# A hybrid network's kernel: its first two layer norms taken on rows of tokens instead of columns

## The chip, the core and the metric

The kernel runs on one core of a Trainium2 chip. A core has engines with a queue of instructions each, which wait for one another by semaphores: TensorE (PE, matmuls and transposes, writing to PSUM; PEld is its weight load), VectorE (DVE), ScalarE (ACT), GpSimd (POOL) and SyncE (SP, which issues DMAs). The metric is the device time of one execution in microseconds (us), as a median of several.

## The reference

A stack of eight blocks on x of shape (4, 1024, 128), in fp32. The change touches the first one, an RWKV mixer. What matters of it:

```python
def _ln(x, g, b):
    m = x.mean(-1, keepdims=True)
    v = x.var(-1, keepdims=True)
    return (x - m) * jax.lax.rsqrt(v + 1e-05) * g + b
...
xn = _ln(x, ln1_g, ln1_b)
xx = _shift(xn)
xk = xn * tm_mu_k + xx * (1.0 - tm_mu_k)
...
k = xk @ Wk
...
x = x + r * wkv @ Wo
ei = _ln(x, ln2_g, ln2_b)
```

Both x in the last but one line and the x under the first norm are themselves the output of a plain layer norm of the input, so the kernel needs two norms of it: an inner one (the residual) and an outer one on top (the mixer's input). Both come from the same mean and variance, since the norm of a norm is the centred input times another factor. wkv is a recurrence over the 1024 tokens of each of the 4 batches; behind it stands the second norm, and then a mixture of experts.

## The kernel before

The 4096 tokens are eight chunks of 512 (`CH`, `NCH`), two for each batch. Nearly everything is kept with the 128 features on partitions and tokens along the free axis: `X` (the input), `Y` (the residual) and `N` (the normed input, padded by a column on each side of a batch). Three fifths of a large buffer, `big[0]` to `big[2]`, serve first for the loaded rows and later for the recurrence's keys K, values V and gates R. Each engine's program is written out by hand in its order; semaphores such as `ln_out` (one more for each chunk of the norm) are counted up through the whole kernel.

The input comes in five DMAs as rows of tokens (`k.rows`, a token on a partition, 128 features along the free axis). TensorE turns each 128x128 tile (`turn`, line 3039) and VectorE copies a turned chunk out of PSUM to `X` (`keep`, line 2990). Then `TwoNorms` runs on columns, in the order that `layernorm` writes out: TensorE multiplies a chunk by a centring matrix (line 89) and the squares (ScalarE, line 96) by a matrix of 1/128 (line 107), so that each column's variance stands on all partitions. ScalarE takes the logarithm twice and the exponential twice (lines 151 to 155, 512 columns each), one pair for the inner and one for the outer norm. VectorE makes the outer norm in two operations (lines 164 and 167) and the inner one, `Y`, in one (line 165). A batch of vectors (gains, biases, mixing factors) is turned in the middle of it, and GpSimd folds the mixing factors into the weights (`rwkv_loads`, lines 394 and 397).

`wkv` follows. TensorE makes keys, values and gates (`mix`, lines 422 and 423), ScalarE takes them out of PSUM (line 474) and makes the recurrence's weights (lines 486 and 488), and VectorE runs the scans and products (lines 540 to 561). On the way out TensorE sums a denominator (`den`, lines 431 and 434), ScalarE inverts it (`over`, lines 492 and 494), VectorE gates (lines 566 and 569), TensorE multiplies by Wo (`out`, line 441), and VectorE adds the product to the residual (`add`, line 584). The second norm's centring (line 89) stands between these in TensorE's queue.

## Time and profile before

| | |
|---|---|
| median of 3 runs | 1082.73 us (1080.31 to 1083.93) |
| the profiled execution's own time | 1089.32 us |
| its span, from the first to the last instruction | 1087.6 us |
| mean granted TensorE clock | 0.959 |
| busy in the span | PE 990.2 us, DVE 845.5 us, ACT 738.1 us, POOL 376.6 us |

The profile is of one execution, and its times count from the span's start. The stages that the change touches take up the first 130 us: the load and the two first norms until about 37 us, the recurrence until about 115 us, the second norm until about 133 us. The busy shares are means over stages with different limits, so they say little of these. Durations are those that the profiler recorded: an instruction that is held up by something inside its engine counts as longer, and one that waits for a semaphore starts later.

### The profile page before, as it was taken

The numbers are of one execution on the slowest core, as the hardware profiler recorded it, in microseconds if no ns is written. First come the engines' busy times: TensorE is split into PE (matmuls) and PEld (weight loads), VectorE is DVE, ScalarE is ACT, GpSimd is POOL, SyncE is SP. The second block draws the span as 40 slices with busy tenths as digits, with TensorE's granted clock in tenths as the row PEclk, the third lists the DMA queues.
The fourth block names the chain that finished last, engine by engine and source line by source line (L and its number), as shares of the span: only waits on it lengthen the run. The fifth ranks groups of instructions, "written<-read, shape, count | busy, mean of one in ns | idle before, by whom it ended". The sixth has DMA issues, their size and how long they took to land.

```text
span 1087.6 us, 21260 instructions
## 1 busy us (share of the span) xinstructions
PE 990.2 (91%) x7772; PEld 634.4 (58%) x7780; DVE 845.5 (78%) x1541; ACT 738.1 (68%) x1313; POOL 376.6 (35%) x480
## 2 busy tenths in 40 slices
PE   7888999889967999899998999889999899898898
PEld 3333544379953544777663454567776777763476
DVE  4899788768745767777765778899879899799974
ACT  5895656546646358455777457788778878886784
POOL 0100037737661113000000113788768777320210
PEclk9998999989989999899999999899889999999989
DMA  7900035368850000000000000000000000000002
GB/s 196 289 16 1 1 112 160 124 220 273 262 183 11 1 0 11 2 2 2 1 1 1 0 1 10 1 3 2 2 2 2 2 27 2 2 1 1 0 1 78
DMA packets 42686, 54.53 MB, mean 50 GB/s; under 512 B 6251, under 2 KB 29244, under 8 KB 42588
## 3 DMA queue, kind: packets, MB, share of 16 engines
q1 hardware_dynamic: 37968, 42.75, 13.3%
q0 software_dynamic: 4288, 10.46, 2.6%
q8 instruction: 62, 1.02, 0.4%
q14 instruction: 36, 0.29, 0.1%
q10 hardware_dynamic: 332, 0.01, 0.0%
HBM read 22.11 MB, written 20.93 MB: 40 GB/s over the span
## 4 chain that ended last, share of the span: by engine, by line
PE 59%; DVE 18%; ACT 12%; issue 7%; DMA 2%; POOL 2%; SPq 0%; ACTq 0%; DVEq 0%
PE psum L1419 4%; PE psum L1391 3%; PE psum L2608 3%; PE psum L2232 3%; PE psum L89 2%; PE psum L1053 2%; PE psum L1019 2%; DVE N L2829 2%; PE psum L1068 2%; DVE arena L2820 2%; ACT N L2720 2%; PE psum L1879 2%; PE psum L1032 2%; PE psum L2618 2%; PE psum L2149 2%
## 5 line engine op out<-in xcount | busy, mean ns | idle before, releaser
L2720 ACT ACTIVATE N<-N 128x1024 f32<-128x1024 f32 x64 | 67.7, 1058 | 27.4 <-DVE N L2829 26.6
L2608 PEld LDWEIGHTS psum<-arena 32*128 32x128 f32 x1024 | 65.8, 196 | 27.0 <-issue 14.9
L2618 PE MATMUL psum<-ident,N 128*128 128x128 f32 x512 | 73.8, 290 | 7.2 <-POOL N L2789 6.5
L2608 PE MATMUL psum<-arena 32*128 32x128 f32 x1024 | 78.4, 293 | 1.6 <-ACT arena L2698 1.4
L2716 ACT ACTIVATE arena<-psum 128x1024 f32<-128x1024 f32 x64 | 65.7, 1027 | 18.1 <-PE psum L2618 17.6
L882 POOL DMA_INDIRECT out_rows<-mixed,out_index x62 | 60.3, 972 | 38.9 <-DVE arena L958 23.3
L1322 POOL TENSOR_TENSOR arena<-arena 128x512 f32<-128x512 f32 x16 | 20.2, 1260 | 138.3 <-DVE arena L1354 138.3
L2789 POOL TENSOR_TENSOR N<-N,arena 128x512 f32<-128x512 f32 x64 | 67.9, 1060 | 0.0
L2783 POOL TENSOR_TENSOR mixed<-N 128x256 f32<-128x256 f32 x64 | 46.7, 730 | 60.9 <-ACT N L2720 60.2
L2618 PEld LDWEIGHTS psum<-ident,N 128*128 128x128 f32 x512 | 58.1, 146 | 16.2 <-POOL N L2789 9.8
L2788 POOL TENSOR_TENSOR N<-N,arena 128x512 f32<-128x512 f32 x64 | 66.9, 1045 | 0.0
L876 POOL DMA_INDIRECT slot_rows<-arena,slot_index x48 | 50.7, 1057 | 28.7 <-ACT arena L822 15.3
L2819 DVE TENSOR_REDUCE arena<-psum 128x8 f32<-128x512 f32 x64 | 43.9, 686 | 21.1 <-PE psum L2608 20.8
L2389 DVE TENSOR_REDUCE arena<-psum 128x32 f32<-128x1024 f32 x32 | 39.1, 1222 | 26.1 <-PE psum L2232 26.1
L1319 POOL MEMSET arena<- 128x512 bf16 x4 | 2.0, 523 | 161.8 <-DVE N L124 161.8
L96 ACT ACTIVATE ln_sq<-psum 128x512 f32<-128x512 f32 x48 | 28.4, 592 | 41.2 <-PE psum L89 40.2
L2337 ACT ACTIVATE arena<-arena 128x1024 f32<-128x1024 f32 x32 | 33.6, 1051 | 21.6 <-DVE arena L2400 21.3
L1419 PE MATMUL psum<-arena,ffw 128*128 128x512 f32 (+1 forms) x96 | 46.8, 625 | 0.0
L2828 DVE TENSOR_TENSOR N<-psum,arena 128x512 f32<-128x512 f32 x64 | 44.2, 691 | 2.2
L89 PE MATMUL psum<-X,center 128*128 128x512 f32 x64 | 37.5, 674 | 8.0 <-DVE X L1176 3.8
L1472 ACT ACTIVATE arena<-psum 9x512 bf16<-9x512 f32 x16 | 9.4, 585 | 52.1 <-PE psum L1403 52.1
L1391 PE MATMUL psum<-arena,ffw 128*128 128x512 f32 x96 | 44.6, 597 | 0.1
(446 smaller groups left out, 2787.7 us busy)
## 6 DMA issues: line engine op xcount, KB each, us to landing
arena<-weights SPq DMA_DIRECT2D x31, 320.0 KB, 2.7
slot_rows<-zeros SPq DMA_DIRECT2D x1, 8060.0 KB, 26.6
arena<-slot_rows SPq DMA_DIRECT2D x31, 260.0 KB
arena<-tw_rows SPq DMA_DIRECT2D x16, 256.0 KB, 3.7
arena<-out_rows SPq DMA_DIRECT2D x6, 512.0 KB
out_dram<-arena SPq DMA_DIRECT2D x8, 256.0 KB, 2.4
arena<-in_L_attn_a_x_dram SPq DMA_DIRECT2D x3, 512.0 KB, 7.1
weights<-in_L_attn_a_eWk_dram SPq DMA_DIRECT2D x1, 1024.0 KB, 5.8
```

The source lines that it names most:

```text
L89: self.nc.tensor.matmul(k.bank[c % W][:], k.center[:], self.src(c), start=True, stop=True).then_inc(k.ln_centered, 1)
L876: nc.gpsimd.indirect_dma_start(k.slot_rows, at, rows[:, t, :], None).then_inc(k.rt_sent, 16)
L882: nc.gpsimd.indirect_dma_start(k.out_rows, at, made[:, i % 4, j, :], None).then_inc(k.sx_out[i % 4], 16)
L1391: nc.tensor.matmul(k.bank[j][:], k.W1[:, j, :], xm[c], start=True, stop=True).then_inc(k.ff_h, 1)
L1419: op = nc.tensor.matmul(own[c][:], k.W2[0:rows, j, :], hm[0:rows, j * CH:(j + 1) * CH], start=(j == 0), stop=(j == GR - 1))
L2608: op = nc.tensor.matmul(scored[half][:, e * P:(e + 1) * P], k.sg_Q[b % 2][at, seg, 2 * j:2 * j + 2, :].rearrange("p h n -> p (h n)"), k.sg ...
L2618: op = nc.tensor.transpose(turned_to[:, e * P:(e + 1) * P], pr[n % 4][:, e * P:(e + 1) * P], k.ident[:])
L2716: nc.scalar.activation(pT[n % 2], turned_to, ACT.Copy).then_inc(k.sg_pT, 1)
L2720: nc.scalar.activation(pr[n % 4], pr[n % 4], ACT.Exp).then_inc(k.sg_exp, 1)
L2783: nc.gpsimd.tensor_tensor(hs[n % 2], mine[:, :, 0:32], mine[:, :, 32:64], ALU.add).then_inc(k.sg_half, 1)
L2788: nc.gpsimd.tensor_tensor(mine, mine, sm[n % 4][:, 0:8, None].to_broadcast([P, 8, SEG]), ALU.mult)
L2789: nc.gpsimd.tensor_tensor(others, others, spread(sm[n % 4][:, 8:40]), ALU.mult).then_inc(k.sg_mul, 1)
```

## The change

`RowNorms` takes the place of `TwoNorms`. It works on the rows as they were loaded, where a token is a partition (for each of four tiles in a chunk) and its 128 features lie along the free axis, so that mean and variance are single numbers per row, kept in a small buffer `row_stats`. For each chunk VectorE sums the rows and scales the sums to means (`mean_rows`); GpSimd subtracts them (`center_rows`, to `big[1]`); ScalarE squares (`square_rows`, to `big[2]`); VectorE sums the squares (`variance_rows`); ScalarE takes two logarithms of 4 columns and one exponential of 8 (`deviation_rows`). VectorE then makes the outer norm from the raw rows, tile by tile with a subtraction and a multiplication by a scalar per row (`scale_outer`, to `big[2]`), TensorE turns the result (`turn`), and ScalarE applies gain and bias on the way to `N` (`affine`). GpSimd makes the inner norm's rows (`scale_inner`), which stay rows in `Y`. The input is still turned for `X`.

The residual is no longer added by VectorE: in `out`, TensorE adds its eight tiles of a batch to PSUM as products with the identity, which turns them, before the product with Wo; `add` only copies. VectorE, and not GpSimd, folds the mixing weights, behind its last chunk. ScalarE's table for the exponentials is loaded behind the decay's exponential. The values wait for the rows of the residual, because they overwrite the centred rows.

```diff
-class TwoNorms(Norm):
-    def __init__(self, nc, k, src, dst, outer, **kinds):
-        super().__init__(nc, k, src, dst, **kinds)
-        self.outer, self.second0 = outer, k.ln_affine * NCH
+class RowNorms(Norm):
...
+    def raw_turned(self, c):
+        return c + 1 + max(0, c - 3)
+    def scaled_turned(self, c):
+        return c + 1 + min(NCH, c + 4)
+    def spread(self, j, c):
+        return self.stat(j, c)[:, :, None].to_broadcast([P, 4, P])
+    def mean_rows(self, dve, c):
         k, nc = self.k, self.nc
-        at = c % W
+        dve.wait_ge(k.loaded[[first <= c < end for first, end in LOADS].index(True)], 16)
+        nc.vector.tensor_reduce(self.stat(0, c), self.rows(k.big[0], c), AX.X, ALU.add).then_inc(k.x_mean, 1)
+        dve.wait_ge(k.x_mean, 2 * c + 1)
+        nc.vector.tensor_scalar(self.stat(0, c), self.stat(0, c), 1.0 / P, None, ALU.mult).then_inc(k.x_mean, 1)
+    def center_rows(self, pool, c):
+        k, nc = self.k, self.nc
+        pool.wait_ge(k.x_mean, 2 * c + 2)
+        nc.gpsimd.tensor_tensor(self.rows(k.big[1], c), self.rows(k.big[0], c), self.spread(0, c), ALU.subtract).then_inc(k.ln_centered, 1)
+    def turn_x(self, pe, c):
+        k, nc = self.k, self.nc
+        pe.wait_ge(k.loaded[[first <= c < end for first, end in LOADS].index(True)], 16)
+        if c >= 4:
+            pe.wait_ge(k.x_ready, c - 3)
+        rows = self.rows(k.big[0], c)
+        for t in range(4):
+            op = nc.tensor.transpose(k.bank[c % 4][:, t * P:(t + 1) * P], rows[:, t, :], k.ident[:])
+        op.then_inc(k.x_turned, 1)
+    def keep_x(self, dve, c):
+        k, nc = self.k, self.nc
+        dve.wait_ge(k.x_turned, self.raw_turned(c))
+        nc.vector.tensor_copy(plain(k.X, c), k.bank[c % 4][:]).then_inc(k.x_ready, 1)
+    def square_rows(self, act, c):
+        k, nc = self.k, self.nc
+        act.wait_ge(k.ln_centered, c + 1)
+        nc.scalar.activation(plain(k.big[2], c), plain(k.big[1], c), ACT.Square).then_inc(k.ln_squared, 1)
+    def variance_rows(self, dve, c):
+        k, nc = self.k, self.nc
+        dve.wait_ge(k.ln_squared, c + 1)
+        nc.vector.tensor_reduce(self.stat(1, c), self.rows(k.big[2], c), AX.X, ALU.add).then_inc(k.ln_var, 1)
...
+        both = k.row_stats[:, 2:4, 4 * c:4 * (c + 1)]
+        act.wait_ge(k.ln_var, c + 1)
+        nc.scalar.activation(self.stat(2, c), self.stat(1, c), ACT.Ln, scale=1.0 / P, bias=k.eps[:, 0:1])
+        nc.scalar.activation(self.stat(3, c), self.stat(1, c), ACT.Ln, scale=(1.0 + EPS_LN) / P, bias=k.eps_eps[:, 0:1]).then_inc(k.ln_logs, 1)
+        act.wait_ge(k.ln_logs, c + 1)
+        nc.scalar.activation(both, both, ACT.Exp, scale=-0.5).then_inc(k.ln_rstd, 1)
...
+    def scale_outer(self, dve, c):
         k, nc = self.k, self.nc
-        at, bank = c % W, k.bank[c % W][:]
-        out = self.outer(c)
+        dve.wait_ge(k.ln_rstd, c + 1)
+        raw, to = self.rows(k.big[0], c), self.rows(k.big[2], c)
+        for t in range(4):
+            op = nc.vector.tensor_scalar(to[:, t, :], raw[:, t, :], self.stat(0, c)[:, t:t + 1], self.stat(3, c)[:, t:t + 1], ALU.subtract, ALU.mult)
+        op.then_inc(k.ln_scaled, 1)
+    def scale_inner(self, pool, c):
+        k, nc = self.k, self.nc
+        pool.wait_ge(k.ln_rstd, c + 1)
+        nc.gpsimd.tensor_tensor(self.rows(k.Y, c), self.rows(k.big[1], c), self.spread(2, c), ALU.mult).then_inc(k.x_rows, 1)
+    def turn(self, pe, c):
+        k, nc = self.k, self.nc
+        if c >= 4:
+            pe.wait_ge(k.ln_out, PRIMED["ln_out"] + c - 3)
+        pe.wait_ge(k.ln_scaled, c + 1)
+        rows = self.rows(k.big[2], c)
+        for t in range(4):
+            op = nc.tensor.transpose(k.bank[4 + c % 4][:, t * P:(t + 1) * P], rows[:, t, :], k.ident[:])
+        op.then_inc(k.x_turned, 1)
...
+        act.wait_ge(k.x_turned, self.scaled_turned(c))
+        nc.scalar.activation(padded(k.N, c), k.bank[4 + c % 4][:], ACT.Identity, scale=k.ln1[:, 0:1], bias=k.ln1[:, 1:2]).then_inc(k.ln_out, 1)
...
+def row_norms(nc, k, block, norm, feed):
+    turn_vecs, keep_vecs = feed
+    k.ln_done, k.ln_logged = NCH + PRIMED["ln_out"], NCH
+    @block.tensor
+    def _(pe):
+        pe.wait_ge(k.ident_one, 1)
+        for c in range(NCH + 3):
+            if c < NCH:
+                norm.turn_x(pe, c)
+            if c == NCH - 1:
+                turn_vecs(pe)
+            if c >= 3:
+                norm.turn(pe, c - 3)
+    @block.scalar
+    def _(act):
+        activations(act, k, "natural_log_exp_and_others")
+        for c in range(NCH + 2):
+            if c < NCH:
+                norm.square_rows(act, c)
+            if 1 <= c <= NCH:
+                norm.deviation_rows(act, c - 1)
+            if c >= 2:
+                norm.affine(act, c - 2)
+    @block.gpsimd
+    def _(pool):
+        for c in range(NCH + 2):
+            if c < NCH:
+                norm.center_rows(pool, c)
+            if c >= 2:
+                norm.scale_inner(pool, c - 2)
+    @block.vector
+    def _(dve):
+        for c in range(NCH + 2):
+            if c < NCH:
+                norm.mean_rows(dve, c)
+            if c >= 2:
+                norm.scale_outer(dve, c - 2)
+            if 1 <= c <= NCH:
+                norm.keep_x(dve, c - 1)
+                norm.variance_rows(dve, c - 1)
+        keep_vecs(dve)
...
-    @block.gpsimd
-    def _(pool):
-        pool.wait_ge(k.wA_in, 64)
-        pool.wait_ge(k.vecs_ready, 1)
+    @block.vector
+    def _(dve):
+        dve.wait_ge(k.wA_in, 64)
+        dve.wait_ge(k.vecs_ready, 1)
         for j, mu in enumerate(("mu_k", "mu_v", "mu_r")):
-            nc.gpsimd.tensor_scalar(k.wmix[:, j, :], k.wA[:, j, :], k.vec(mu), None, ALU.mult).then_inc(k.mix_fold, 1)
+            nc.vector.tensor_scalar(k.wmix[:, j, :], k.wA[:, j, :], k.vec(mu), None, ALU.mult).then_inc(k.mix_fold, 1)
         for j in range(3):
-            pool.wait_ge(k.mix_fold, j + 1)
-            nc.gpsimd.tensor_tensor(k.wA[:, j, :], k.wA[:, j, :], k.wmix[:, j, :], ALU.subtract).then_inc(k.mix_fold, 1)
+            dve.wait_ge(k.mix_fold, j + 1)
+            nc.vector.tensor_tensor(k.wA[:, j, :], k.wA[:, j, :], k.wmix[:, j, :], ALU.subtract).then_inc(k.mix_fold, 1)
...
-                pe.wait_ge(k.ln_out, normed - NCH + 1 + (W + n if n < W else 2 * b + c))
+                pe.wait_ge(k.ln_out, normed - NCH + 1 + 2 * b + c)
...
+            pe.wait_ge(k.x_rows, 2 * b + 2)
+            for t in range(8):
+                nc.tensor.matmul(backs[b][:, t * P:(t + 1) * P], rows[:, 8 * b + t, :], k.ident[:], start=(t % 4 == 0), stop=False, skip_group_check=True)
             pe.wait_ge(k.wkv_out, b + 1)
             for c in range(2):
-                nc.tensor.matmul(backs[b][:, c * CH:(c + 1) * CH], k.wA[:, 3, :], R[:, half[b][c]], start=True, stop=True).then_inc(k.wkv_prod, 1)
+                nc.tensor.matmul(backs[b][:, c * CH:(c + 1) * CH], k.wA[:, 3, :], R[:, half[b][c]], start=False, stop=True, skip_group_check=True).then_inc(k.wkv_prod, 1)
...
-        activations(act, k, "exp_and_others")
...
+                if kind == "V":
+                    act.wait_ge(k.x_rows, 2 * b + c + 1)
...
+        activations(act, k, "exp_and_others")
...
-                nc.vector.tensor_tensor(k.Y[:, half[b][c]], k.Y[:, half[b][c]], backs[b][:, c * CH:(c + 1) * CH], ALU.add).then_inc(k.wkv_y, 1)
+                nc.vector.tensor_copy(k.Y[:, half[b][c]], backs[b][:, c * CH:(c + 1) * CH]).then_inc(k.wkv_y, 1)
...
-    layernorm(k, block, first, feed)
+    row_norms(nc, k, block, first, feed)
...
+    def turn_vecs(pe):
+        pe.wait_ge(k.x_ready, 5)
+        pe.wait_ge(k.vecs_in, 16 * len(table))
+        nc.tensor.transpose(late[:, 0:len(VROWS)], k.vrows[:], k.ident[0:len(VROWS), 0:len(VROWS)]).then_inc(k.vecs_turned, 1)
```

The first place is VectorE's program of the first norms. In the kernel before, it does this for a chunk, here ahead of the copy of the turned vectors (`vecs`; `N` and `Y` are the two results):

```order
L2990 COPY X<-psum 128x512
L164 SCALAR_TENSOR_TENSOR N<-psum,ln,arena 128x512
L165 TENSOR_TENSOR Y<-psum,ln_std 128x512
L167 TENSOR_SCALAR N<-N,ln 128x512
L3063 COPY vecs<-psum 128x43
```

Three operations out of PSUM and one in place made a chunk of both results and of `X`. In the changed kernel the same engine does this for a chunk in the middle of the stage (line numbers are now the changed kernel's own, and `arena` holds the rows):

```order
L161 TENSOR_REDUCE row_stats<-arena 128x4
L163 TENSOR_SCALAR row_stats<-row_stats 128x4
L211 TENSOR_SCALAR arena<-arena,row_stats 128x128 x4
L183 COPY X<-psum 128x512
L193 TENSOR_REDUCE row_stats<-arena 128x4
```

Only the copy to `X` is left of the former operations; the scalings (line 211) are those of the chunk two ahead of the one that is summed in line 161. The second place is the end of the same stage on VectorE:

```order
L183 COPY X<-psum 128x512
L193 TENSOR_REDUCE row_stats<-arena 128x4
L211 TENSOR_SCALAR arena<-arena,row_stats 128x128 x4
L3157 COPY vecs<-psum 128x43
L505 UNCONDITIONAL_BRANCH
L510 TENSOR_SCALAR mixed<-wA,vecs 128x128 x3
L513 TENSOR_TENSOR wA<-wA,mixed 128x128 x3
```

The copy of the vectors and the folding of the mixing weights have moved behind the last scaling. The third place is TensorE's program on the way out of the recurrence. Before, the sums of batch 2 (lines 431 and 434), the product of batch 0 (line 441) and the sums of batch 3 follow on one another:

```order
L431 MATMUL psum<-ln_std,ident 128x512 x2
L434 MATMUL psum<-ln_sq,ident 128x512 x2
L441 MATMUL psum<-arena,wA 128x512 x2
L431 MATMUL psum<-arena,ident 128x512 x2
L434 MATMUL psum<-arena,ident 128x512 x2
```

Nothing but these stands between the sums. In the changed kernel the former lines 431, 434 and 441 are lines 548, 551 and 561:

```order
L548 MATMUL psum<-ln_std,ident 128x512 x2
L551 MATMUL psum<-ln_sq,ident 128x512 x2
L558 MATMUL psum<-ident,Y 128x128 x8
L561 MATMUL psum<-arena,wA 128x512 x2
L548 MATMUL psum<-arena,ident 128x512 x2
L551 MATMUL psum<-arena,ident 128x512 x2
```

Line 558, the eight tiles of the residual, has come in ahead of the product, and so it does for each of the four batches.

## Rows read from the trace of the kernel before

**Rows 1.** Windows: busy us of each engine (instructions), granted clock, DMA share, GB/s.
```profile
15.00:35.70 20.70, 16.06 (x43) 6.23 (x42) 14.89 (x25) 19.93 (x36) 5.04 (x23) 1.00 0.75 210
90.00:95.00 5.00, 1.98 (x3) 0.83 (x3) 4.93 (x5) 4.69 (x5) 0.00 (x0) 0.76 0.00 0
95.00:100.00 5.00, 5.00 (x8) 2.08 (x7) 4.93 (x5) 1.24 (x2) 0.00 (x0) 0.56 0.00 0
```

**Rows 2.** Chain of waits, end of the first norms: start, us, what.
```profile
35.16 0.53 ACT arena L155
...
38.31 2.30 DVE arena L540
```

**Rows 3.** Chain of waits, the way out of the recurrence.
```profile
93.23 3.78 PE psum L431 x4
...
99.99 1.72 PE psum L441 x4
101.70 1.72 PE psum L431 x4
...
106.85 1.73 PE psum L89 x4
...
112.68 1.95 PE psum L441 x4
```

**Rows 4.** Timeline, two instructions: start, us, engine, line, operation [idle before, releaser].
```profile
6.12 1.28 ACT L46 ACT_TABLE_LOAD   x1 [6.12 <-issue]
...
112.68 0.67 PE L441 MATMUL psum<-arena,wA 128*128 128x512 f32 x1 [0.68 <-DVE arena L569]
```

**Rows 5.** Single lines: count, duration in ns as min/median/max, first and last start, forms.
```profile
L2836 DVE TENSOR_REDUCE arena<-N x64: 673/676/685, 692.0 to 933.9; 128x32 f32<-128x512 f32 x64
L1295 DVE TENSOR_SCALAR ffw<-ffw,W_sum x3: 275/279/285, 347.8 to 348.2; 128x128 f32<-128x128 f32 x2, 96x128 f32<-96x128 f32 x1
L326 DVE TENSOR_SCALAR weights<-weights x3: 169/170/174, 941.6 to 1048.1; 128x4 f32<-128x4 f32 x2, 128x16 f32<-128x16 f32 x1
L2990 DVE COPY X<-psum x8: 682/691/692, 5.8 to 23.9; 128x512 f32<-128x512 f32 x8
L2788 POOL TENSOR_TENSOR N<-N,arena x64: 1035/1045/1061, 693.9 to 936.6; 128x512 f32<-128x512 f32 x64
L271 ACT ACTIVATE mixed<-X x8: 612/624/682, 776.9 to 946.9; 128x512 f32<-128x512 f32 x8
L295 ACT ACTIVATE weights<-psum,eps x7: 244/246/274, 783.2 to 1030.1; 128x4 f32<-128x4 f32 x6, 128x16 f32<-128x16 f32 x1
```

**Rows 6.** Timeline of VectorE at 347.8 us.
```profile
347.84 0.67 DVE L1295 TENSOR_SCALAR ffw<-ffw,W_sum 128x128 f32<-128x128 f32 x3
```

**Rows 7.** Timeline of VectorE and GpSimd at 360 us and at 990 us.
```profile
360.31 0.48 DVE L1266 TENSOR_SCALAR arena<-N,vecs 128x512 f32<-128x512 f32 x1
360.48 1.21 POOL L1322 TENSOR_TENSOR arena<-arena 128x512 f32<-128x512 f32 x1 [27.80 <-DVE arena L1354]
360.83 1.41 DVE L1268 SCALAR_TENSOR_TENSOR arena<-N,vecs,arena 128x512 f32<-128x512 f32 x1
...
989.71 1.42 POOL L1531 TENSOR_TENSOR ln_sq<-X 128x512 f32<-128x512 f32 x1 [2.87 <-DVE X L1903]
990.15 1.52 DVE L1557 TENSOR_TENSOR Y<-X,ln_std 128x512 f32<-128x512 f32 x1
```

**Rows 8.** Single lines of VectorE, columns as in rows 5.
```profile
L1268 DVE SCALAR_TENSOR_TENSOR arena<-N,vecs,arena x16: 750/1293/1409, 331.7 to 639.1; 128x512 f32<-128x512 f32 x16
L167 DVE TENSOR_SCALAR N<-N,ln x8: 476/478/1265, 17.5 to 37.0; 128x512 f32<-128x512 f32 x8
L2538 DVE TENSOR_SCALAR arena<-psum,vecs x4: 742/744/751, 680.6 to 685.1; 128x512 f32<-128x512 f32 x4
```

**Rows 9.** Timeline of TensorE in the last store.
```profile
1072.38 1.95 PE L1917 MATMUL psum<-weights,X 128*128 128x128 f32 x16
...
1074.17 1.04 PE L1938 MATMUL psum<-ident,arena 128*128 128x128 f32 x8
```

More of the change, by code:

```diff
@@ L147, in deviation @@
         if c == 0:
             act.wait_ge(k.consts_set, 6)
-        act.wait_ge(k.ln_var, self.n0 + c + 1)
-        var = k.bank[W + c % self.vary][:]
-        nc.scalar.activation(k.ln_std[:, at, :], var, ACT.Ln, bias=k.eps[:, 0:1])
-        nc.scalar.activation(k.ln_std2[:, at, :], var, ACT.Ln, scale=1.0 + EPS_LN, bias=k.eps_eps[:, 0:1]).then_inc(k.ln_logs, 1)
-        act.wait_ge(k.ln_logs, self.n0 + c + 1)
-        nc.scalar.activation(k.ln_std[:, at, :], k.ln_std[:, at, :], ACT.Exp, scale=-0.5)
@@ L155, in deviation @@
-        nc.scalar.activation(k.ln_std2[:, at, :], k.ln_std2[:, at, :], ACT.Exp, scale=-0.5).then_inc(k.ln_rstd, 1)
-    def scale(self, dve, c):
-        k, nc = self.k, self.nc
-        at, bank = c % W, k.bank[c % W][:]
-        out = self.outer(c)
-        if c == 0:
-            dve.wait_ge(k.ln1_in, 32)
-        dve.wait_ge(k.ln_rstd, self.n0 + c + 1)
-        nc.vector.scalar_tensor_tensor(out, bank, k.ln1[:, 0:1], k.ln_std2[:, at, :], ALU.mult, ALU.mult).then_inc(k.ln_scaled, 1)
-        nc.vector.tensor_tensor(self.dst(c), bank, k.ln_std[:, at, :], ALU.mult)
-        dve.wait_ge(k.ln_scaled, self.second0 + c + 1)
-        nc.vector.tensor_scalar(out, out, k.ln1[:, 1:2], None, ALU.add).then_inc(k.ln_out, 1)
+        both = k.row_stats[:, 2:4, 4 * c:4 * (c + 1)]
@@ L170, with affine @@
+    def affine(self, act, c):
+        k, nc = self.k, self.nc
+        if c == 0:
+            act.wait_ge(k.ln1_in, 32)
+            act.wait_ge(k.pads_set, 2 * B)
+        act.wait_ge(k.x_turned, self.scaled_turned(c))
+        nc.scalar.activation(padded(k.N, c), k.bank[4 + c % 4][:], ACT.Identity, scale=k.ln1[:, 0:1], bias=k.ln1[:, 1:2]).then_inc(k.ln_out, 1)
 class CentredNorm(Norm):
@@ L2920, in favor_out @@
         pe.wait_ge(k.fv_x, c + 1)
-    return [TwoNorms(nc, k, X, Y, N, enter=loaded, vary=2),
+    return [RowNorms(nc, k),
             Norm(nc, k, Y, N, gain="ln2_g", bias="ln2_b", enter=mixed_out, clear=mixed_free),
@@ L2978, in load @@
         ("b1_0", row(a["L0_ffn_bo1"]))]
-    late = k.bank[6]
+    late = k.bank[0]
     def vectors(eng, first):
@@ L3030, in _, with keep_vecs @@
         nc.vector.tensor_tensor(k.center[:], k.ident[:], k.mean[:], ALU.subtract).then_inc(k.center_set, 1)
[L3031 to L3066 removed]
+    def turn_vecs(pe):
+        pe.wait_ge(k.x_ready, 5)
+        pe.wait_ge(k.vecs_in, 16 * len(table))
+        nc.tensor.transpose(late[:, 0:len(VROWS)], k.vrows[:], k.ident[0:len(VROWS), 0:len(VROWS)]).then_inc(k.vecs_turned, 1)
+    def keep_vecs(dve):
+        dve.wait_ge(k.vecs_turned, 1)
+        nc.vector.tensor_copy(k.vecs[:], late[:, 0:len(VROWS)]).then_inc(k.vecs_ready, 1)
+        dve.wait_ge(k.vecs_ready, 1)
+    return turn_vecs, keep_vecs
 def store(nc, k, block, out):
@@ L3198, in build @@
         with nc.Block() as block:
-            loaded, *feed = load(nc, k, block, a)
-            norms = all_norms(nc, k, loaded)
+            feed = load(nc, k, block, a)
+            norms = all_norms(nc, k)
             with ExitStack() as own:
```

52 lines of the change are left out of this document (13 added, 39 removed).

## The prediction

> **What bounds the kernel now.** I began with the windows. From 15 us to the end of the first two norms at 35.7 us ScalarE is busy 19.93 of 20.70 us, while VectorE has 14.89 and TensorE 16.06 [rows 1]. The chain of waits agrees: its last link before VectorE takes over is ScalarE's second exponential at 35.16 us, and VectorE's first scan of the recurrence starts at 38.31 us [rows 2]. So the first stage is ScalarE's, and its price is the time at which that scan can start. From there VectorE works through the recurrence's chain; the change leaves that work as it is, and whatever moves the scan moves it whole. The second place is the way out of the recurrence. There the chain stands on TensorE: 93.23 us, 99.99 us, 101.70 us, 106.85 us, until the last output product at 112.68 us [rows 3], ahead of which TensorE was idle for only 0.68 us [rows 4]. Anything put into TensorE's queue in this stretch is paid for, but for those 0.68 us.
>
> **The sum's base.** The profiled execution took 1089.32 us (span 1087.6 us), 0.6% above the median of 1082.73 us. I work out a difference on the trace and add it to both.
>
> **What the first stage loses and gains.** Ln and Exp now work on four or eight columns (0.25 us each [rows 5]) instead of 512, so ScalarE no longer bounds it. VectorE's queue for a chunk of 512 tokens becomes: one reduction (0.676 us), a small multiply (0.17 us), four scalings of 128x128 (0.279 us each alone), one copy out of PSUM (0.691 us) and a second reduction (0.676 us) [rows 5]. Three independent scalings together took 0.67 us [rows 6], so each adds 0.195 us after the first and four take 0.87 us; in the same way an operation that follows without a dependence starts some 0.08 us before the recorded end of the one ahead. The sum is 3.08 us of durations less four overlaps of 0.08 us, plus some 0.03 us for each of four waits: **2.9 us per chunk if nothing disturbs it**.
>
> Something does. GpSimd gets two tensor operations of 128x512 for each chunk, 1.045 us each [rows 5], and the centring of a chunk is released by the very multiply after which VectorE starts the four scalings; the residual's rows follow at once, as their standard deviation is long there. The rows show what the two engines do to each other: a scaling of VectorE that began at 360.31 us kept its 0.48 us, GpSimd's operation began at 360.48 us and took 1.21 us, and VectorE's next operation, begun at 360.83 us, took 1.41 us [rows 7] where its undisturbed length is 0.750 us [rows 8]. It got going at 361.49 us, some 0.85 us after GpSimd had been let in (1.045 us ahead of its end at 361.69 us). At 989.71 us GpSimd got in between two VectorE operations that don't depend on each other, and the second took 1.52 us [rows 7]. That a plain scaling with one tensor input is stopped too is shown by line 167: 0.478 us in the median, 1.265 us where GpSimd was at work [rows 8]. So I take it that one VectorE operation and one GpSimd operation alternate, and that each GpSimd operation stops VectorE for 0.85 us: scaling, centring, scaling, residual rows, two scalings. The price is 1.7 us per chunk, and the pace **4.6 us**. Reductions and PSUM copies I take as undisturbed (line 2836 stays between 0.673 and 0.685 us [rows 5], in a stage full of GpSimd operations).
>
> The Trainium skill ("SBUF — State Buffer", section "Who interferes with whom") speaks against this change as well: a VectorE scaling from SBUF to SBUF takes the port pair shared with GpSimd, whoever is second stands still for the whole instruction, and a reduction never contends. Here the rows agree on who stands still; by "the whole instruction" the price would be two times 1.045 us per chunk, and the forecast 3 us longer.
>
> **When the scan starts.** The first square waits for ScalarE's table load, which ends at 7.40 us [rows 4]; with the square (0.624 us) and the reduction behind it [rows 5] VectorE takes up chunk 2 at 8.7 us. Chunks 2 to 7 at 4.6 us: 36.3 us. Then nothing is left to fill the waits: Ln, Ln, Exp 0.75 us, scaling of chunk 6 with GpSimd's share 1.72 us, copy and reduction 1.25 us, Ln, Ln, Exp 0.75 us, scaling of chunk 7 1.72 us: 42.5 us. The vectors' copy and the folding of the mixing weights, which moves from GpSimd to VectorE (three scalings 0.67 us, three sums of about the same, the copy and waits 0.25 us), end at 44.1 us. Only now can TensorE make the first keys: before, they were made under the norm. Two chunks are four passes of 128x512, 1.72 us at the upper clock and 3.78 us where it was low [rows 3]. In the forecast TensorE has eight transposes every 4.6 us (eight take 1.04 us [rows 9]) and waits some 3.5 us in between; in the trace before, a wait of 3.0 us ahead of 93.23 us came with a granted clock of 0.76 and then 0.56 [rows 1], so I take the low level (1.2 GHz). With the pipeline's end, ScalarE's copy (as long as the square) and semaphores, 0.9 us, the scan starts at 48.8 us instead of 38.31 us: **10.5 us later**. With the clock up it would be 46.75 us.
>
> Hidden, and so costed at nothing: the affine on ScalarE, one operation of 512 columns per chunk in a queue that is now mostly empty; the table load of 1.28 us, which moves behind the decay's exponential and lies beside folding and keys; the zeroed rows' DMA, issued by SP once GpSimd has made the zeros, later than now, but read by nothing before the experts; and the values' wait for the residual's rows, which are made by 42.5 us.
>
> **What the way out of the recurrence pays.** The residual is now added by TensorE: ahead of each batch's product stand eight 128x128 products with the identity, in fp32 with new weights each. The same shape stands in the store at the end: sixteen passes from 1072.38 us until the next operation at 1074.17 us [rows 9], 1.79 us for eight. Four batches are 7.16 us. They stand behind the sums of batch 2 in TensorE's queue, so TensorE's wait ahead of 93.23 us can't hide them. VectorE's copy in place of its sum saves nothing: either moves 512 columns out of PSUM, in about 0.69 us. The wait of 0.68 us ahead of 112.68 us is filled [rows 4]: the two batches ahead of it delay the second norm's first centring, and with it ScalarE and VectorE, by 3.6 us; TensorE itself, with two more groups of 1.79 us, comes still later. So the last product starts **6.5 us later**, and the second norm's variances, queued behind it, with it. Nothing later gives this back, as the chain runs on over engines.
>
> Sum: 10.5 + 6.5 = **17.0 us** slower: 1106.3 us profiled, **1099.7 us** as a median.
>
> **Rivals.**
> 1. *The two-pointer scaling is single-rate.* The scalings here read two scalars per row, which no scaling from SBUF in the trace does. At one element per cycle it would not meet GpSimd. The nearest row for the slower rate is line 2538, 0.744 us for 512 columns out of PSUM [rows 8], which at 384 columns less and 0.96 columns per ns is 0.344 us for 128: 0.26 us more per chunk, pace 3.16 us. The scan then starts at 37.2 us with TensorE, fed every 3.2 us, at the upper clock, 39.2 us without. With 6.5 us: 5.4 to 7.4 us slower, **1088 to 1090 us**. Against it: line 1295's 0.279 us is a two-element rate with one scalar [rows 5].
> 2. *GpSimd's operations slip under VectorE's reductions and copies; the other side.* In each chunk 1.9 us of VectorE's work does not meet GpSimd's 2.1 us. If the scalings get through ahead of the centring, the pace is 2.9 us, TensorE never waits 3 us, and the scan starts at 34.85 us, 3.45 us earlier; less 6.5 us, that is 3.05 us slower, **1085.8 us**, which is not told from no change. It decides at a scan at 35.0 us or earlier. Against it: centring and scaling are released together, and GpSimd got in between two VectorE operations at 989.71 us [rows 7].
> 3. *Dearer than forecast.* If GpSimd stops VectorE for its full 1.045 us, that is 0.4 us for each of eight chunks, 3.2 us; if the clock is still low when the first residual products run, another 1.8 us: **1104.7 us**.
>
> **How the numbers follow.** Forecast (1094 to 1102 us) 0.66, rival 1 0.13, rival 2 0.09, rival 3 0.07; the rest, 0.05, is for a stage that ends earlier than any of these. The measurement tells some 0.3%, 3.2 us, from no change; of rival 2 and of what lies about it 0.09 falls within that, and 0.05 is faster: faster 0.05, same 0.09, slower 0.86. The range runs from rival 2's edge, 1085 us, to rival 3, 1105 us; the forecast's own is 1094 to 1102 us.
>
> **What would show it.** Right: VectorE's scalings, a mean of 0.5 us or more where 0.28 us would be undisturbed; the chain on VectorE between 9 and 42 us; the first scan near 48.8 us; four groups of sixteen passes of 1.8 us on TensorE before the second norm. Wrong: scalings of 0.28 to 0.35 us with a pace near 3 us (rival 1 or 2); a first scan ahead of 40 us; or TensorE waiting between those groups, so that the residual products were free.

## The result and the profile after

Median of the changed kernel: 1109.66 us (1102.09 to 1114.79), of the kernel before on the same chip 1083.33 us (1080.31 to 1084.85): ratio 1.0217, 95% interval 1.0175 to 1.0259. It is slower, as forecast, but by 26.3 us where 17.0 were forecast, and above the range's end of 1105 us. The profiled execution took 1112.88 us (span 1111.1 us), 23.5 us more than that of before.

The chain of waits follows the work that ended last back through whatever released it. In the changed kernel it runs through the first stage like this (start, length, engine and what it writes; one chunk, then the end of the stage; an fp32 matmul of 512 columns shows as two passes, x2):

```profile
14.32 2.71 DVE arena L211 x4
...
19.02 2.71 DVE arena L211 x4
...
37.82 1.93 DVE arena L211 x4
...
41.73 2.35 DVE arena L211 x4
...
45.18 0.61 DVE wA L513 x3
...
45.83 2.07 PE psum L539 x2
47.91 1.71 PE psum L540 x2
49.61 1.71 PE psum L539 x2
51.32 0.94 PE psum L540 x2
52.29 0.60 ACT arena L595
...
52.99 2.30 DVE arena L662
```

A chunk costs 19.02 - 14.32 = 4.70 us on VectorE (4.6 forecast), of which the four scalings (line 211) are 2.71. The scan that stood at 38.31 us [rows 2] now stands at 52.99: 14.7 us later, not 10.5. The last 7.2 us ahead of the scan are not the norm at all: TensorE makes the first keys (lines 539 and 540) and ScalarE takes them, in series behind the folded weights. Their first passes take 1.71 us for two, later ones 0.86: TensorE's clock has two levels, 1.2 and 2.4 GHz (a granted clock of 0.50 and 1.00), and these ran at the lower one. The trace's first record of the granted clock stands only at 51.3 us, so a view's 1.00 ahead of it says nothing; the times do. In the kernel before, four transposes of 128x128 took 1.06 us until about 10.7 us and 0.60 us from there; in the changed kernel four still took 1.08 us at 44.23 us. TensorE, with transposes and waits alone ahead of the keys, stayed at the lower level through the whole stage.

VectorE's first scaling of the chunk and what GpSimd does meanwhile, in the timeline, then GpSimd at the last chunk:

```profile
19.02 1.21 DVE L211 TENSOR_SCALAR arena<-arena,row_stats 128x128 f32<-128x128 f32 x1
19.10 1.04 POOL L168 TENSOR_TENSOR arena<-arena,row_stats 128x512 f32<-128x512 f32 x1 [2.66 <-DVE row_stats L163]
20.10 1.04 POOL L217 TENSOR_TENSOR Y<-arena,row_stats 128x512 f32<-128x512 f32 x1
...
41.78 1.04 POOL L217 TENSOR_TENSOR Y<-arena,row_stats 128x512 f32<-128x512 f32 x1 [2.88 <-ACT row_stats L204]
42.76 0.32 POOL L740 MEMSET zeros<- 128x260 f32 x1
```

The first scaling of the four had begun 0.08 us before the centring (line 168), and yet it is the one that is held until that ends: 1.21 us. The second, behind the residual's rows (line 217), takes 1.08, the other two 0.33 each. The statistics of the line (shortest, median and longest in ns) are:

```profile
L211 DVE TENSOR_SCALAR arena<-arena,row_stats x32: 332/368/1704, 9.7 to 43.7; 128x128 f32<-128x128 f32 x32
```

The way out of the recurrence, from the chain of waits again; [rows 3] had 93.23, 99.99 and 112.68 for the first of these links, the first product, and the last:

```profile
107.90 1.98 PE psum L548 x4
109.88 1.72 PE psum L551 x4
111.60 1.78 PE psum L558 x16
113.38 1.72 PE psum L561 x4
...
128.98 1.78 PE psum L558 x16
130.76 1.72 PE psum L561 x4
```

The denominators of batch 2 (lines 548, 551) start 14.7 us later, as the scan does. They take 3.70 us, 6.76 before: TensorE's granted clock was 1.00 over them here, and 0.76 and 0.56 in the trace of before [rows 1]. The residual's products (line 558) are 1.78 us, four times, with no wait between. So the last output product should be 14.7 - 3.1 + 7.1 - 0.7 = 18.0 us later, where 0.7 is the wait that is filled; it is 18.1: 130.76 against 112.68. From there to the end, in stages that the change leaves alone, the lag grows to 23.5 us.

### The profile page after: what moved, and what is told of

Read it like the earlier page. It is cut to its first block, busy times and chain, and to the rows that moved or that the text cites. A ratio compares the mean times of both kernels' runs of the same rounds, so it can differ in the third digit from the quotient of the medians.

```text
span 1111.1 us, 21440 instructions
## 1 busy us (share of the span) xinstructions
PE 995.8 (90%) x7844; PEld 648.0 (58%) x7844; DVE 863.8 (78%) x1579; ACT 731.4 (66%) x1313; POOL 392.0 (35%) x490
## 3 DMA queue, kind: packets, MB, share of 16 engines
q1 hardware_dynamic: 37968, 42.75, 12.9%
## 4 chain that ended last, share of the span: by engine, by line
PE 56%; DVE 20%; ACT 11%; issue 7%; POOL 3%; DMA 1%; ACTq 0%; SPq 0%; DVEq 0%
PE psum L1541 4%; PE psum L1513 3%; PE psum L2730 3%; PE psum L2354 3%; PE psum L1175 2%; PE psum L1190 2%; POOL slot_rows L998 2%; PE psum L89 2%; ACT N L2842 2%; PE psum L2740 2%; DVE arena L211 2%; DVE N L2951 2%; DVE arena L2942 2%; PE psum L2001 2%; PE psum L1141 2%
## 5 line engine op out<-in xcount | busy, mean ns | idle before, releaser
L2730 PEld LDWEIGHTS psum<-arena 32*128 32x128 f32 x1024 | 66.6, 198 | 26.3 <-issue 15.9
L2905 POOL TENSOR_TENSOR mixed<-N 128x256 f32<-128x256 f32 x64 | 46.7, 730 | 63.0 <-ACT N L2842 62.2
L96 ACT ACTIVATE ln_sq<-psum 128x512 f32<-128x512 f32 x40 | 23.7, 592 | 41.4 <-PE psum L89 40.3
L2942 DVE TENSOR_REDUCE arena<-psum 128x32 f32<-128x512 f32 x64 | 43.5, 679 | 0.0
```

Of the source, the lines that this page charges most:

```text
L2730: op = nc.tensor.matmul(scored[half][:, e * P:(e + 1) * P], k.sg_Q[b % 2][at, seg, 2 * j:2 * j + 2, :].rearrange("p h n -> p (h n)"), k.sg ...
L2905: nc.gpsimd.tensor_tensor(hs[n % 2], mine[:, :, 0:32], mine[:, :, 32:64], ALU.add).then_inc(k.sg_half, 1)
L2942: nc.vector.tensor_reduce(mx[n % 2][:, 8:40], others, AX.X, ALU.max).then_inc(k.sg_max, 1)
```

## The experiments

Theory after the profile: GpSimd's two operations per chunk each stop one VectorE scaling (pace); the first keys stand in series behind the norm; the residual's products cost TensorE what they last. Main rival: the two-pointer scalings are slow by themselves. Marks of time below are of the profiled executions. "Out" is the start of the last output product in the chain of waits: 112.68 us in the kernel before, 130.76 in the changed one, whose scans start at 38.31 and 52.99.

**GpSimd behind the scalings.**

```diff
 def center_rows:   pool.wait_ge(k.x_mean, 2 * c + 2)
+                   if c >= 2: pool.wait_ge(k.ln_scaled, c - 1)
 def scale_inner:
-                   pool.wait_ge(k.ln_rstd, c + 1)
+                   pool.wait_ge(k.ln_scaled, c + 1)
```

> Changed kernel with GpSimd's two operations on a chunk released only after VectorE's four scalings, so that they run beside the copy and the two sums. Theory (a GpSimd operation stops VectorE's two-pointer scalings, and nothing else of its loop): the 32 scalings 0.33 us each with a longest under 0.6, the pace 2.06 + 1.3 = 3.3 us a chunk in place of 4.70, scan 8 to 9 us earlier, at 44 to 45 us, run 7 to 10 us shorter than the changed kernel. Rival (the scalings are slow by themselves, or the sums and copies are stopped as well): pace at least 4.3 us, scan after 51 us.

Timeline and statistics of this kernel (its line 213 is 211 of the changed kernel):

```profile
20.50 1.12 DVE L213 TENSOR_SCALAR arena<-arena,row_stats 128x128 f32<-128x128 f32 x4 [0.29 <-ACT row_stats L206]
...
22.73 0.68 DVE L161 TENSOR_REDUCE row_stats<-arena 128x4 f32<-128x512 f32 x1
23.44 0.39 DVE L163 TENSOR_SCALAR row_stats<-row_stats 128x4 f32<-128x4 f32 x1
24.12 1.11 DVE L213 TENSOR_SCALAR arena<-arena,row_stats 128x128 f32<-128x128 f32 x4 [0.29 <-ACT row_stats L206]
...
44.97 2.29 DVE L664 TENSOR_TENSOR_SCAN arena<-diff,arena 128x1024 f32<-128x1024 f32 x1 [5.76 <-ACT arena L597]
```
```profile
L213 DVE TENSOR_SCALAR arena<-arena,row_stats x32: 340/343/347, 9.7 to 35.2; 128x128 f32<-128x128 f32 x32
```

All 32 scalings now take 0.34 us; four take 1.11 instead of 2.71. GpSimd's operations (1.04 us as ever, from 21.76 and 22.76 us) now lie beside the copy and the two reductions, whose 0.68 us hardly change. The pace is 3.61 us, not 3.3, because the edit ties a chunk into a chain: scalings (20.50 us), centring (21.76), square (22.84), logarithms and exponential, and the next scalings at 24.12 us, for which VectorE waits 0.29 us. The small multiply (line 163) meets GpSimd and takes 0.39 instead of 0.17, but that lies ahead of the wait. The scan is 8.0 us earlier, in the bounds of the theory. Up to the first pass of the keys it is 7.5 us (38.31 for 45.83), although the folding's three scalings now meet GpSimd's last row operation and take 1.67 instead of 0.68 us; the other 0.5 us came from TensorE's clock, which rose earlier among the keys' passes (5.93 us). Median 1101.61 us, ratio to before 1.0173 (1.0094 to 1.0251).

**One GpSimd operation per chunk instead of two.**

```diff
-for c in range(NCH + 2):
-    if c < NCH: norm.center_rows(pool, c)
-    if c >= 2: norm.scale_inner(pool, c - 2)
+for c in range(NCH): norm.center_rows(pool, c)
+for c in range(NCH): norm.scale_inner(pool, c)
```

> Changed kernel with GpSimd's second operation on each chunk (the residual's rows) moved behind its eight centrings, so that one operation a chunk falls on the scalings. Theory (each operation stops one scaling for 0.75 us): pace 4.70 - 0.75 = 3.95 us a chunk, one scaling of four at about 1.1 us, scan 4 to 5 us earlier, at about 48.5 us. Rival (the stop is by chunk and not by operation, or GpSimd is the pace): pace still at 4.5 or more, or down to 3.3.

Its timeline, VectorE and then GpSimd:

```profile
21.51 1.97 DVE L211 TENSOR_SCALAR arena<-arena,row_stats 128x128 f32<-128x128 f32 x4
...
25.47 1.98 DVE L211 TENSOR_SCALAR arena<-arena,row_stats 128x128 f32<-128x128 f32 x4
...
29.43 4.20 DVE L211 TENSOR_SCALAR arena<-arena,row_stats 128x128 f32<-128x128 f32 x4
```
```profile
29.52 1.04 POOL L168 TENSOR_TENSOR arena<-arena,row_stats 128x512 f32<-128x512 f32 x1 [2.92 <-DVE row_stats L163]
30.51 7.02 POOL L217 TENSOR_TENSOR Y<-arena,row_stats 128x512 f32<-128x512 f32 x7
```

The pace is 3.96 us: the four scalings last 1.11 us with no GpSimd operation, 1.97 with one, 2.71 with two, so 0.86 and 0.74 us for each. Where GpSimd's seven postponed operations run, all four scalings are stopped (4.20 us). That burst falls on the stage's end, so the scan gains only 1.3 us (51.67): my 48.5 forgot it. Median 1102.54 us, ratio 1.0176 (1.0108 to 1.0243).

**The first keys ahead of the last turn.** The folding moves ahead of the scalings of chunks 6 and 7 in VectorE's loop, and:

```diff
 # TensorE                      # ScalarE
 mix("K", 0)                    take("K", 0)
+norm.turn(pe, NCH - 1)        +norm.affine(act, NCH - 1)
 mix("K", 1) ...                take("K", 1)
```

> Changed kernel with the weights folded on VectorE one chunk earlier and the first K's passes put ahead of the turn of the last chunk, its take ahead of the last affine step (the kernel before had these passes inside its norms). Theory (of the 14.7 us that the scan came later, 6.4 + 0.6 are these passes and their take standing in series behind the norm): passes from about 40.5 to 47 at the lower clock level, scan at 47.5 to 48.5 and 4.5 to 5.5 us earlier than in the changed kernel. Rival (the norm's own end sets the scan whatever the order): scan not before 51.

Timeline of TensorE, then VectorE:

```profile
40.35 1.09 PE L226 MATMUL psum<-ident,arena 128*128 128x128 f32 x4 [3.28 <-DVE arena L211]
41.23 1.92 PE L541 MATMUL psum<-N,mixed 128*128 128x512 f32 x2
42.94 1.09 PE L542 MATMUL psum<-N,wA 128*128 128x512 f32 x2
43.87 1.02 PE L541 MATMUL psum<-N,mixed 128*128 128x512 f32 x2
44.73 1.02 PE L542 MATMUL psum<-N,wA 128*128 128x512 f32 x2
```
```profile
42.19 2.35 DVE L211 TENSOR_SCALAR arena<-arena,row_stats 128x128 f32<-128x128 f32 x4 [0.80 <-ACT row_stats L204]
...
46.48 2.29 DVE L667 TENSOR_TENSOR_SCAN arena<-diff,arena 128x1024 f32<-128x1024 f32 x1 [1.09 <-ACT arena L599]
```

The norm's own end is where it was, its last scalings even 0.5 us later, and yet the scan is 6.5 us earlier: the keys' passes now lie beside those scalings. The forecast, 47.5 to 48.5, was too late, since the clock rose early here: eight passes in 4.30 us, 2.1 less than in the changed kernel, so that by this estimate some 2 of the 6.5 us are the clock's. "Out" moved 5.0 us, to 125.75: the gates' passes ahead of the denominators met the lower level here (granted clock 0.57 from 87 to 91 us). Median 1100.95 us, ratio 1.0123 (1.0078 to 1.0167).

**Idle matmuls to keep TensorE's clock up.**

```diff
+if NCH - 1 <= c <= NCH + 1:
+    ...
+    for _ in range(3):
+        nc.tensor.matmul(k.bank[1][:, 0:256], k.ident[:], k.X[:, 0:256], start=True, stop=True)
```

> Changed kernel with nine idle matmuls of 128x256 on TensorE between its last turns (three behind each of the turns of chunks 4, 5 and 6, where it waits 2.8 to 3.6 us), into a bank that is overwritten. Theory (the eight passes of the first K are slow because TensorE came to them at the lower clock level, 1.9 us for two passes): the eight passes take 3.4 us in place of 6.44, at a granted clock of 1.00, and the first scan starts 3.0 us earlier, at 50.0. Rival (the passes wait on something else, operands or weights): still over 6 us and scan at 53.

Timeline of TensorE, then a window (length, busy us of PE, PEld, DVE, ACT and POOL, granted clock, DMA share, GB/s):

```profile
40.51 1.46 PE L416 MATMUL psum<-X,ident 128*128 128x256 f32 x6
44.37 0.63 PE L226 MATMUL psum<-ident,arena 128*128 128x128 f32 x4 [2.40 <-DVE arena L211]
45.97 1.39 PE L543 MATMUL psum<-N,mixed 128*128 128x512 f32 x2 [0.98 <-DVE wA L517]
47.16 1.92 PE L544 MATMUL psum<-N,wA 128*128 128x512 f32 x2
```
```profile
46.70:50.10 3.40, 3.40 (x5) 1.35 (x4) 0.12 (x1) 1.10 (x2) 0.00 (x0) 0.50 1.07 341
```

A miss. The turn at 44.37 us does run at the upper level (0.63 us where the changed kernel has 1.08), but behind the waits of 2.40 and 0.98 us the level fell, 0.7 us after the passes had begun: the eight passes take 5.4 us, and the scan is at 52.10. Passes at 1.9 us for two are the lower level all the same: the granted clock was 0.50 from 46.7 to 50.1 us, and pairs of 1.02 us follow from 50.35 us on. So the rival, that they wait on operands or weights, falls with this run. Median 1101.82 us, ratio 1.0149 (1.0105 to 1.0194).

**Without the residual's products.**

```diff
-pe.wait_ge(k.x_rows, 2 * b + 2)
-for t in range(8):
-    nc.tensor.matmul(backs[b][:, t * P:(t + 1) * P], rows[:, 8 * b + t, :], k.ident[:], ...)
-... k.wA[:, 3, :], R[:, half[b][c]], start=False, ...
+... k.wA[:, 3, :], R[:, half[b][c]], start=True, ...
```

> Changed kernel without the residual's 32 matmuls of 128x128 (four times 1.78 us, 7.1 us in all): the residual is left out of the output. Theory (the products lie on TensorE's path and cost what they last): scan still at 53.0 us, the first denominator matmul of batch 2 still at 107.9, the last output product's start at 130.8 - 7.1 = 123.7, and the whole run about 7 us shorter than the changed kernel. Rival (they fill TensorE and so keep its clock up, and are partly paid back): the denominators and products around 94 to 130 us show a granted clock under 1.00, and less than 5 us come back.

Scan 52.11, denominators of batch 2 from 107.03 us, "out" at 125.11. From the one to the other are 18.1 us, against 130.76 - 107.90 = 22.9 in the changed kernel: 4.8 us less. The denominators took 5.4 us here, 1.7 more than there, and TensorE waits 0.7 us ahead of the last product again: 4.8 + 1.7 + 0.7 = 7.2 us for the products. The rival's signs came true as well: less than 5 us came back, and the granted clock over the denominators was 0.68. But the denominators stand ahead of the first of these products, and in two executions that have the products (GpSimd behind the scalings, and the idle matmuls) they took 5.4 us too, so the level can't be put down to their absence. Median 1102.07 us, ratio 1.0158 (1.0084 to 1.0231).

**The same products in the kernel before**, eight matmuls of 128x128 ahead of each output product, which overwrites them:

> Kernel before with the same 32 matmuls of 128x128 put ahead of the output products, into banks that the product overwrites (the output is the reference's). Theory: the last output product starts at 112.68 + 7.1 - 0.7 (a wait that it takes up) = 119.1 if the denominators of batch 2 take 6.76 us as before, or up to 3 us earlier if TensorE runs there at the upper clock; the whole run 6 to 7 us over the kernel before, 1.006. Rival (hidden beside other work): under 2 us.

"Out" at 118.88 us, 6.2 us later, with 1.78 us for each group of sixteen passes in the chain of waits, and the denominators of batch 2 at 6.72 us as in the kernel before. Median 1088.10 us, ratio 1.0049 (1.0015 to 1.0082): 4.0 us, less than the 6 to 7 forecast, which lie within the interval.

**The products of batches 0 and 1 moved ahead of the denominators.**

```diff
+back(0)        # the eight matmuls alone
+back(1)
 den(2)
 out(0)
```

> Changed kernel with the residual's matmuls of batches 0 and 1 (1.78 us each) moved ahead of the denominators of batch 2, into the 3.02 us for which TensorE waits there. Theory: the denominators of batch 2 start about 1.0 later (108.9), and the last output product 3.56 - 1.0 = 2.5 us earlier, at 128.2 if the denominators run at the upper clock level as in the changed kernel (3.7 us). Rival (the matmuls only push the denominators back by their own length): last output product within 0.5 us of 130.8.

```profile
105.42 3.84 PE L558 MATMUL psum<-ident,Y 128*128 128x128 f32 x32 [0.69 <-ACT arena L601]
109.10 1.88 PE L548 MATMUL psum<-ln_std,ident 128*128 128x512 f32 x4
...
128.18 1.88 PE L565 MATMUL psum<-arena,wA 128*128 128x512 f32 x4
```

"Out" at 128.34, 2.4 us earlier, as forecast (2.3 against its own scan at 52.84). Median 1100.37 us, ratio 1.0121 (1.0075 to 1.0168).

**The changed kernel once more.**

> The changed kernel once more. What the profile showed beyond the two stages that the change touches (17.8 us later at the second norm, 23.5 at the end). Theory (in the stages behind, TensorE's clock level falls now here and now there, in every run otherwise): the second norm again 17 to 21 us later by its own denominators, but the shift behind it grows or shrinks at other places than before, by up to 5 us, and single runs spread over 10 us; the median of the runs 16 to 23 us over the kernel before. Rival (the shift itself costs something fixed in a stage behind, such as the 3.4 us at the first experts): the same steps at the same places, and an end 23 us or more later again.

Chain of waits, the first keys again:

```profile
45.78 2.08 PE psum L539 x2
47.85 1.56 PE psum L540 x2
49.41 0.86 PE psum L539 x2
50.27 0.87 PE psum L540 x2
```

The same passes, 5.36 us in place of 6.43: the clock rose earlier. "Out" was at 131.33, 18.7 us later than before, and the span 1099.3 us, 11.7 us longer than before's, where the first profile had 18.1 and 23.5. So the lag *shrank* by 7 us behind the recurrence in one execution and grew by 5 in the other. Both are counted from the one profiled execution of before, which is itself 6 us over its median. Six runs: median 1104.84 us (1101.07 to 1111.26) against 1085.57, ratio 1.0181 (1.0144 to 1.0219).

**A delay and nothing else, in the kernel before.**

```diff
-nc.vector.tensor_copy(k.lam, ...)
+for i in range(26):
+    nc.vector.tensor_copy(k.lam, ...).then_inc(k.wkv_init, 1)
+    dve.wait_ge(k.wkv_init, 3 + i)
```

> Kernel before with nothing but a delay: VectorE fills the recurrence's constant row 26 times in place of once, 25 times 0.72 us, so that the scan starts 18.0 us later, about as far as the changed kernel's last output product came later. It asks whether a shift costs more than itself in the stages behind. Theory (the lag that grew from 18.1 to 23.5 us in one execution of the changed kernel, and shrank in another, is run-to-run): scan at 56.3, median 16 to 20 us over the kernel before. Rival (stages behind fit worse to a shifted start): median 21 to 27 us over the kernel before.

```profile
36.42 18.90 DVE L580 COPY diff<-wneg 128x1024 f32<-128x1024 f32 x26
55.36 2.29 DVE L540 TENSOR_TENSOR_SCAN arena<-diff,arena 128x1024 f32<-128x1024 f32 x1
```

Scan 17.0 us later, "out" at 128.36, 15.7 us later with the denominators of batch 2 at 3.70 us as in the changed kernel. Median 1102.37 us against 1084.52: 17.9 us, ratio 1.0169 (1.0121 to 1.0218). The interval is 13 to 24 us: a shift costs about itself, 2.2 us more than "out" moved in the profiled execution.

**The causes together, and the banks of the denominators.** First GpSimd behind the scalings, the first keys early and the products ahead of the denominators:

> Changed kernel with three edits together: GpSimd's operations behind the scalings, the first K's passes ahead of the last turn with the weights folded one chunk earlier, and the residual's matmuls of batches 0 and 1 ahead of the denominators of batch 2. Theory (the three causes are separate and add): scan at 52.99 - 8.0 - 6.5 = 38.5, at most 41 if the passes find the lower clock level; last output product 2.4 us earlier against the scan than in the changed kernel, so at about 114 to 116.5 in place of 112.68; the median of the runs 2 to 7 us over the kernel before. Rival (they overlap, since one wait hides the other): scan after 43 and the run over 10 us slower than the kernel before.

Scan 40.05, within the forecast; "out" 117.19 and the median, 1089.53 us (7.6 us over, ratio 1.0064, 1.0035 to 1.0094), a little past it. The two gains of the first stage, 8.0 and 6.5 us, sum to 14.5, and 12.9 were found. "Out" stands 77.1 us behind its scan, only 0.6 less than in the changed kernel, as the first of the gates' passes ran at the lower level (granted clock 0.50 from 82 to 85 us). Of the 4.5 us by which "out" is still later than before, 1.7 are the scan's; the rest lies on TensorE, where the residual's products are left. Second, an idea that the wait of 3.02 us ahead of the denominators suggests, in the kernel before:

```diff
-totals = [k.pair[2], k.pair[3]]
-backs = [k.pair[0], k.pair[1], k.pair[2], k.pair[3]]
+totals = [k.pair[2], k.pair[3], k.pair[0], k.pair[1]]
+backs = [k.pair[2], k.pair[3], k.pair[2], k.pair[3]]
-den(2); out(0); den(3); out(1)
+den(2); den(3); out(0); out(1)
...
```

The waits of both change with the banks, and ScalarE's reciprocal of batch 3 (`over(3)`) moves ahead of the second norm's first squares; this run doesn't part them.

> Kernel before, with the denominators of batches 2 and 3 in the banks that the last mixes leave (they then wait only for the takes, and not for the logarithm of batch 0, 3.02 us in the trace of before), both ahead of the first output product, and the output products in the two pairs of banks that the first denominators leave. Theory (TensorE's wait of 3.02 us, and its low clock level behind it, hold up the four results; without it VectorE's own work of 15 rows sets the end of the stage): denominators of batch 2 at 90.2 in place of 93.23, last output product at 107 to 109 in place of 112.68, median 3 to 6 us under the kernel before. Rival (VectorE's results wait for the reciprocals in the same order anyway): last output product within 1 us of 112.7, no change of time.

```profile
89.74 1.88 PE L431 MATMUL psum<-ln_std,ident 128*128 128x512 f32 x4
...
107.34 1.95 PE L441 MATMUL psum<-arena,wA 128*128 128x512 f32 x4
```

"Out" at 107.42, 5.3 us earlier, the denominators at the upper level. Median 1079.71 us against 1081.90, 2.2 us less where 3 to 6 were forecast, ratio 0.9971 (0.9935 to 1.0006): the fastest kernel of the study, though by the interval not told from the kernel before. Third, the same banks in the changed kernel with the first two edits:

> Changed kernel with GpSimd's operations behind the scalings, the first K's passes ahead of the last turn, and the banks of the denominators changed as in the version of the kernel before. Theory: scan at 38.5 to 41; TensorE has slack for the residual's four times 1.78 us once the denominators stand ahead, so the last output product is set by VectorE and comes 69.5 + 2 us behind the scan, at 110 to 113; median from 3 us under the kernel before to 4 us over it. Rival (the residual's matmuls fill TensorE whatever the order): last output product 75 us behind the scan or later, at 114 to 117.

"Out" 116.21, 76.2 us behind its scan at 40.03: the rival's figure. From 93.62 us on the chain stands on TensorE without a wait: with four more groups of 1.78 us it has no slack in this order either. Median 1090.47 us, ratio 1.0071 (1.0033 to 1.0108).

## Why the prediction was right and wrong

**Right: the mechanism and the sign.** VectorE bounds the first stage and GpSimd stops its scalings, once per operation; pace 4.70 against 4.6 (four scalings alone 1.11 us instead of 0.87, the two stops 1.60 instead of 1.70), chunk 2 taken up at 8.74 against 8.7. In the forecast's order the first scaling went free and the second and third were stopped; the trace has the first and second stopped. Reductions and PSUM copies are not stopped. The residual's products cost 1.78 us for each batch against 1.79, and the 0.68 us ahead of the last product was filled.

**Luck: the local sum, 18.1 us against 17.0.** The scan's term was 4.2 us too small (14.7 for 10.5) and the way out's 3.1 us too large (3.4 for 6.5). The two errors below nearly cancel.

**Mis-sized: "Two chunks are four passes of 128x512, 1.72 us at the upper clock and 3.78 us where it was low".** Each chunk has two matmuls of two passes each, so two chunks are eight passes: 6.43 us, and 5.36 in the second execution; at the upper level, where the chain has 0.86 us for two, it would be 3.44. That is 2.7 us of the 4.2 by which the scan came later than forecast. The level itself was forecast rightly; by the transposes' times TensorE had been at the lower one all along. Another 1.7 us, less 0.2 in the take, stand at the stage's end: VectorE was done with chunk 7's reduction 0.7 us late, the scalings of chunks 6 and 7 took 1.93 and 2.35 us instead of 1.72. Behind GpSimd's row operation at 41.78 us come its memsets from 42.76 us, which the forecast did not have in the way.

**Not foreseen: the denominators' clock.** I kept the 6.76 us of [rows 3]. They ran at the upper level and took 3.70, which gave back 3.1 us. In six further executions, of the changed kernel and its variants, with the same wait of 3.02 us ahead, they took 3.7 us (three times) or 5.4 us (three times, granted clock 0.68). The wait alone does not fix the level.

**Wrong: "I work out a difference on the trace and add it to both."** This is the step that put the median past the range. The sum was to be carried to the end whole ("Nothing later gives this back"), with some 0.3% as what a measurement can tell. Behind the recurrence the lag moved by +5 us in one execution and by -7 us in the other of the same kernel, in stages the change does not touch; the ten runs of the changed kernel reach from 1101.07 to 1114.79 us. The range allowed for the unknown costs, and nothing for this. The median was 8 us over the local sum in the first set (26.3 against 18.1), 1 us in the second (19.3 against 18.7), and 2 us with the bare delay (17.9 against 15.7). What goes with the 8 us is the runs' own mean granted clock: in the first set two of four runs stood at 0.957 (1112.88 and 1114.79 us), while at 0.966 the changed kernel took 1106.43 us in the first set and 1103.76 and 1104.88 in the second. Over its ten runs time and clock go together (correlation -0.95), by about 1 us for each 0.001; no run here sets the clock, so that it is the cause is argued and not shown. So most of the 8 us belongs to that set of four runs and not to the change. At 0.967 the changed kernel has one run of 1102.09 us and the kernel before, in the later sets, thirteen with a mean of 1082.3; straight lines through its ten runs and through 61 of the kernel before are 22 us apart at 0.965. By this estimate the change costs 20 to 22 us at equal clock; whether the 2 to 4 us over the local sum are tied to the shift, or to how the stages behind met it, stays open.

**The rivals.** Rival 1 had the price of a two-pointer scaling right, 0.344 us against 0.343 measured without GpSimd, and its conclusion wrong: such a scaling does meet GpSimd. (By its own terms its scan stands at 36.9 us, not 37.2.) Whether 0.34 is a slower rate or a longer fixed part can't be told from one size. Rival 2 fell: the scalings never got through first. Rival 3's full 1.045 us per stop was too much: 0.86 and 0.74.

## What to carry to other kernels

Before work is moved to GpSimd, see which VectorE operations it is released beside: next to reductions and PSUM copies it was free, next to SBUF scalings it cost 0.8 us for each 1.04 us operation, and two changed waits took that away, but for 1.0 us where the last operation then met the folding. When a stage is rewritten, list what used to run under it: the first keys, no longer under the norm, cost 6.5 us, some 2 of them by the clock's level; all of GpSimd's stops gave back 8.0. A local sum can come out within a microsecond, even by luck, and the whole run still lie 8 us off it, so a range needs that width of its own. Runs compared at the same mean granted clock lay closer together.

## What the runs showed of the hardware that was not expected

VectorE and GpSimd alternate operation by operation even when GpSimd has seven in a row (four scalings 4.20 us), and a VectorE operation on four columns is stopped as well (0.39 us instead of 0.17, with GpSimd behind the scalings). The Trainium skill ("SBUF — State Buffer", section "Who interferes with whom") has the one who comes second stand still for the whole instruction; here, by the recorded starts, the scaling that was held had begun 0.08 us before GpSimd's operation, the stop was 0.86 us for the first and 0.74 us for the second operation of 1.04 us, and the reductions did not contend (0.67 and 0.68 us), as that page says.

The same eight passes behind the norm took 6.43 and 5.36 us in two executions of one kernel, and 5.4 us where idle matmuls had brought TensorE to the upper level before a wait. The view of the granted clock reads 1.00 where the trace has no record of it: in the changed kernel for the first 51.3 us, in which passes took twice as long as later ones.
